# Twelve probability buffers, and fewer, longer value passes in two stages of a four-stage attention kernel

## The reference

```
x = x + masked_attention(layernorm(x))      # softmax over keys j >= i
x = x + ffn0(layernorm(x))                  # one of 8 matrices, picked by an argmax
x = x + rbf_attention(layernorm(x))         # exp(-sigma * |q - k|^2), no softmax
x = x + ffn0(layernorm(x))
x = x + relative_attention(layernorm(x))    # QK + uK + rel_shift(Qr + vr), softmax
x = x + ffn1(layernorm(x))
x = x + rope_attention(layernorm(x))        # rotated q and k, softmax
x = x + ffn1(layernorm(x))
```

## Time and profile before

| | |
|---|---|
| median of 3 runs | 2841.02 us |
| profiled execution | 2840.0 us, span 2838.2 us |
| PE busy | 2662.1 us (94%) |
| DVE busy | 2066.8 us (73%) |
| ACT busy | 2100.8 us (74%) |
| GpSimd busy | 905.8 us (32%) |
| value matmuls (L977) | 30208 instructions |

### The profile page before, as it was taken

One profiled execution on the slowest core, in us unless ns is written; L12 is line 12 of the kernel. 1 busy time (PEld: TensorE's weight loads), 2 busy tenths in 40 slices (PEclk: granted clock), 3 DMA queues, 4 the chain that ended last, 5 costly groups with the idle time before them and its releaser, 6 DMA issues.

```text
span 2838.2 us, 107110 instructions
## 1 busy us (share of the span) xinstructions
PE 2662.1 (94%) x43744; PEld 1599.3 (56%) x43744; DVE 2066.8 (73%) x5515; ACT 2100.8 (74%) x3766; POOL 905.8 (32%) x1609
## 2 busy tenths in 40 slices
PE   3999998999999999999999999999999999999995
PEld 1666565655555555666666666666644444444443
DVE  4888888822222228888788888878889989999992
ACT  1777776799999996666666666666678878888883
POOL 2212132322213242722541361252136134351231
PEclk7999999999999999999999999999999999999997
DMA  6333232334424351411331241222123223232121
GB/s 175 88 95 116 85 109 79 112 104 127 128 88 121 96 160 55 125 57 55 97 89 50 72 131 50 72 81 70 45 64 106 63 63 98 64 112 63 57 71 40
DMA packets 197778, 250.62 MB, mean 88 GB/s; under 512 B 48340, under 2 KB 113748, under 8 KB 197288
## 3 DMA queue, kind: packets, MB, share of 16 engines
q1 hardware_dynamic: 197288, 243.77, 29.2%
HBM read 133.28 MB, written 100.14 MB: 82 GB/s over the span
## 4 chain that ended last, share of the span: by engine, by line
PE 69%; DVE 20%; issue 5%; ACT 2%; SPq 2%; DMA 1%; POOL 1%; DVEq 0%; ACTq 0%; POOLq 0%
PE ppv L977 29%; DVE mx L1244 14%; PE ring L834 6%; PE ring L884 6%; PE ring L819 5%; PE ring L845 4%; PE ring L917 3%; PE pm L1013 2%; DVE seen L1228 2%; DVE seen L1239 1%; PE ring L933 1%; PE pm L998 1%; PE pm L1067 1%; PE pm L1058 1%; ACT probs L1118 1%
## 5 line engine op out<-in xcount | busy, mean ns | idle before, releaser
L1118 ACT ACTIVATE probs<-ring 128x512 f32<-128x512 f32 (+1 forms) x3280 | 1969.8, 684 | 662.9 <-PE ring L834 316.0
L1244 DVE TENSOR_REDUCE mx<-ring 128x1 f32<-128x512 f32 (+2 forms) x2112 | 1284.0, 649 | 241.7 <-PE ring L884 89.4
L977 PE MATMUL ppv<-probs,values 128*32 128x128 f32 x30208 | 1146.9, 278 | 7.3 <-POOL probs L1511 2.8
L977 PEld LDWEIGHTS ppv<-probs,values 128*32 128x32 f32 x30208 | 792.8, 109 | 321.2 <-issue 163.6
L1239 DVE CUSTOM_DVE_ANT_0 seen<-ring,low_seen 128x512 f32<-128x512 f32 x576 | 392.4, 681 | 72.0 <-PE ring L884 71.6
L891 PE MATMUL ring<-kst,qst 48*128 48x512 bf16 (+1 forms) x1060 | 362.6, 391 | 37.7 <-DMA kst<-records_k 20.0
L845 PE MATMUL ring<-qst,kst 51*128 51x512 bf16 (+2 forms) x1092 | 346.2, 385 | 15.8 <-issue 11.5
L1481 POOL CAST mparts<-mall 128x8 bf16<-128x8 f32 x192 | 36.6, 191 | 826.0 <-DVE mall L1262 700.6
L884 PE MATMUL ring<-kst,qst 112*128 112x512 bf16 (+3 forms) x768 | 251.6, 328 | 11.8 <-DVE mx L1228 6.7
L1511 POOL TENSOR_SCALAR_AFFINE_SELECT probs<-probs 128x512 f32<-128x512 f32 x128 | 81.3, 635 | 564.9 <-ACT probs L1118 352.0
L834 PE MATMUL ring<-qst,kst 115*128 115x512 bf16 (+3 forms) x768 | 250.9, 327 | 0.0
(11 more groups left out here) (165 smaller groups left out, 3002.5 us busy)
## 6 DMA issues: line engine op xcount, KB each, us to landing
qst<-records_q SPq DMA_DIRECT2D x448, 96.0 KB
heads_out<-osb SPq DMA_DIRECT2D x256, 128.0 KB, 2.0
kst<-records_k SPq DMA_DIRECT2D x320, 96.0 KB
records_k<-parts SPq DMA_DIRECT2D x96, 256.0 KB, 3.2
records_q<-parts SPq DMA_DIRECT2D x96, 256.0 KB, 3.4
kst<-records_k SPq DMA_DIRECT2D x128, 102.0 KB
oT<-heads_out SPq DMA_DIRECT2D x64, 128.0 KB, 2.7
den<-inverses SPq DMA_DIRECT2D x48, 128.0 KB, 2.6
```

What stands on the lines that cost most here:

```text
L977: mm = pe.matmul(ppv[32 * g:32 * g + 32, c:c + P], values[:, (n // H) % 2, v:v + 32], src[:, at * P:(at + 1) * P], start=u == 0 and qt < 4 ...
L1118: nc.scalar.activation(probs_of(rd.n, u), src, ACT.Exp, scale=1.0 if rd.s == RBF else SCALE).then_inc(s_exp, 1)
L1244: ins = dve.tensor_reduce(mx[:, slot, to:to + 1], bank[:, at * P:(at + nt) * P], AX.X, ALU.max)
```

## The change

NBUF goes from 8 to 12. In REL the four passes of a round become three, of seven, six and five units, behind slots 8, 14 and 20. In MASKED the three passes become two, of five and four units, behind slots 6 and 11. The number of value matmuls is the same. Two more things follow from NBUF: the buffer of a narrow unit is its number modulo 12, and in the first narrow round after the wide rounds of RBF the first 12 units, not the first 8, wait for the pass of the unit three to four before them. The wide rounds go on using the first eight buffers, in four pairs.

```diff
-NBUF = 8
+NBUF = 12
...
     if rd.s == REL:
-        return {6: [0, 1, 2, 3, 4], 10: [5, 6, 7], 14: [8, 9, 10, 11, 12], 20: [13, 14, 15, 16, 17]}
+        return {8: [0, 1, 2, 3, 4, 5, 6], 14: [7, 8, 9, 10, 11, 12], 20: [13, 14, 15, 16, 17]}
     if n == 9:
-        return {5: [0, 1, 2], 8: [3, 4, 5], 11: [6, 7, 8]}
+        return {6: [0, 1, 2, 3, 4], 11: [5, 6, 7, 8]}
```

## The result

In four runs of each, taking turns on one chip, the changed kernel took 2881.36 us (2875.85 to 2891.4) and the kernel before 2842.65 us (2840.93 to 2856.81): a ratio of 1.0134, interval 1.0103 to 1.0165. The forecast was 2849 us, the range ended at 2860. The sign was right, the size five times too small.

The account below looks back on a forecast made before the run. Quiet rounds were taken as a loop through PE and DVE, coupled by three PSUM banks. Terms +10.0 - 2 + 2.6 - 3.8 + 1 = +7.8 us gave 2847.8 in a profile, 2849 us as median; range 2825 to 2860.

Parts of the forecast that it names:

- Step 1: Buffers: twelve instead of eight bring nothing by themselves; they let passes wait longer.
- Step 2: PE: each pass costs 0.23 us beside its units; 64 masked and 64 relative rounds lose one each, 29.4 us.
- first rival: Whole kernel: PE is the bound and the switch price is simply saved, 29.4 us less, 2812 us; chance 10%.
- Step 3: Quiet relative rounds: new waits for DVE at slots 7 and 8 outweigh the saving; +0.25 us each, +10.0 for 40.
- Step 5: Quiet masked rounds: one DVE idle grows to 0.77 us, the other shrinks to 0.15; +0.08 each, +2.6 for 32.
- Steps 4 and 6: Loaded rounds: relative ones mostly escape new waits, -2 us; many masked ones save the full price, -3.8 us.
- Step 7: Seams at the first wide round and first narrow round after: each 0 to 0.8–1.2 us, together +1 us.
- last rival: Masked stage: passes outrun ScalarE, each waiting 0.3 us for an exponential; +19 us more, 2862 or more; chance 10%.

Follow-up runs that it names:

- e1: Kernel before with twelve buffers and all passes where they were: 2840.48 us against 2841.37, ratio 1.0000.
- e7: Changed kernel with maxima reading 32 columns of each bank and not subtracted, exponential scale 1e-6: 2725.59 us, ratio 0.9587 to the kernel before.
- e8: e7 with the relative stage's transpose moved to slot 8, beside the seven-unit pass: 2714.49 us, measured once.
- e4: Changed kernel with ScalarE's planned work of a slot, the emptying of pm in it, ahead of the exponential: 2870.71 us against 2842.87, ratio 1.0100.
- e5: Kernel before with ScalarE's planned work of a slot, the emptying of pm in it, ahead of the exponential: 2837.39 us, ratio 0.9983.
- e10: e7 with masked exponentials reading and writing 256 of 512 columns: 2711.69 us, measured once.
- v1: Kernel before with twelve buffers, emptying first, and four evener relative passes (first two of four units each): 2837.79 us against 2841.79, ratio 0.9988.
- v2: Kernel before with twelve buffers, emptying first, four evener relative passes, masked passes and eviction a slot later: 2842.91 us against 2844.03, ratio 0.9993.

## Why the prediction was wrong

**Step 1, buffers:** right (e1).

**Step 2, the price of a pass:** the 0.23 us is real on PE (0.21 from e7 to e8), but counted one time too many. I took it as saved in all 128 rounds; in the relative ones it had been shared with the transpose, and parting the two brings it back. So the first rival, 29 us of gain, was not to be had even with a quick DVE: with quick maxima the relative round is 13.76 either way, and the chance of 10% was generous. Step 3 did not suffer much, since it walked PE's own timeline.

**Step 3, quiet relative rounds:** right, mechanism and size: +0.21 us a round for +0.25. The waits at slots 7 and 8 were 0.14 and 0.16 for 0.22 and 0.17, the pass 1.67 for 1.67, DVE's idle before slot 9 1.15 for 1.04. One term of the walk was too small: it put slot 7 0.06 us behind the transpose, and it came 0.15 behind (1267.81 to 1267.96). The wait for DVE that follows is shorter by as much, so the sum did not feel it. e7 shows that it is DVE's loop: with quick maxima the loss is gone.

**Step 5, quiet masked rounds, is the step that failed first:** +13.1 us for +2.6. Its first half is right (0.82 idle for 0.77). The failing words are "the other idle shrinks to some 0.15, since slots 7 to 2 run with no pass between". The stretch ends at slot 3, not at slot 2. The second pass stands behind slot 2 and grew from three units to four; slot 3's item comes behind it, and that idle is 0.49. 6.08 + 0.82 + 0.49 gives 7.39 by the very method of the step; it was not taken round the whole loop. Nor was this pass priced: it takes 1.43 us, where the price of step 2 for four units gives 0.14 + 4 x 0.218 = 1.01.

**Steps 4 and 6, loaded rounds:** wrong in sign, +6.0 and +8.7 us for -2 and -3.8. "PE has no gap" was read as "PE saves the full price". A PE without gaps says that nothing makes it wait now, not how near the next wait is. In the masked stage it was in the emptying of `pm`, which the pass behind slot 8 had covered; e4 and e5 show that this is 5.5 of the 6.3 us that the 25 rounds at full clock lose. The rest of the masked row is the seam (1.6), and what the granted clock and the count of rounds make of it. In the relative stage the order gives back 2.6 us in the changed kernel (e4) but 1.6 in the kernel before too (e5), so about 1 of the 6.0 is its doing; the rest I put down to DVE's loop, since with quick maxima 1.6 is left, but no single wait of it was traced.

**Step 7, seams:** the first wait came as the step has it, between the last two masked evictions (8.94 us for 7.37, in the loaded row of the table). ACT of the changed kernel, then of the kernel before, at the first wide exponentials:

```profile
604.38 2.85 ACT L1118 ACTIVATE probs<-ring 128x1024 f32<-128x1024 f32 x3 [1.64 <-PE ppv L977]
```

```profile
580.10 2.86 ACT L1118 ACTIVATE probs<-ring 128x1024 f32<-128x1024 f32 x3 [0.74 <-PE ring L819]
```

It cost 1.6 us, where the step allowed 1.2 at the most. The other +4.7, and the 2.5 before the first eviction, the step did not have. Much of it goes with the granted clock: 0.83 from 605 to 615 us, where the same place before (580 to 590) had 1.00, and 0.79 from 1118 to 1126 for 1.00 (1091 to 1099). e4, with the same passes and the clock at 1.00, takes 6.49 us from the last masked eviction to the first of RBF, as the kernel before does, and the changed kernel takes 7.86. What set the clock back in these places was not tried; it stays open. The second seam of the step, at the end of RBF, costs nothing that shows (501.7 for 501.9).

The last rival, passes that outrun ACT, had the right engine and the wrong place. In the rounds read here no pass waits inside for an exponential; ACT holds up PE's scores through the ring (e7, e10) and the projections through the emptying (e4). Its 2862 was nearest to the 2881 of all that was listed. Of the 38.7 us, then: quiet rounds of both stages 21.5, loaded masked 8.7 (a seam of 1.6 in it), loaded relative 6.0, the rest the other seams and the clock. The trace's differences add up to 43, since the profiled execution of the changed kernel, 2883.0 us, lies 1.6 above its median, and that of the kernel before 2.7 below the median here.

The Trainium skill (Perfetto Trace Analysis, Matmul Optimizations) wants matmuls back to back in batches, because the matmul engine scales its power with its utilization. Here the granted clock was already 1.00 in the quiet rounds of both kernels and 0.99 over the masked stage, so the longer batches had nothing to win, and they cost 1.3%. Its other advice there, to use all 8 PSUM banks, is followed already: six in `ring`, and `pm` and `ppv`. PE's passes turn into idle time at the two rings of three; no run had a larger ring.

## What to carry to other kernels

When a producer serves engines through a ring of a few banks and goes away for a burst, go once round the whole loop for each served engine: burst, plus the time until its next item, less the work that the ring holds for it; a burst that the ring's work does not cover leaves such an idle, and lengthening one at the edge of its cover gives the added length as idle (v1: 0.22 us more of pass, 0.21 of idle). A saved switch is worth nothing if another instruction beside it was sharing its price. A burst can also cover another engine's work: before taking it away, ask what is done beneath it. Here it was an emptying of PSUM that stood in program order behind an exponential; putting it in front took the wait away. And before two sums of rounds are called equal, look at the granted clock of each round in them.

## What was unexpected of the hardware

- A transpose of 24 weight columns between bf16 score matmuls costs PE 0.25 us beyond the 0.22 us steps of its neighbours, as much as a pass of f32 value matmuls costs beside its units; next to each other they cost it once (13.76 and 13.55 us a round, e7 and e8).
- The DMA that places the maxima is close behind PE: with masked rounds of 6.85 us instead of 7.02, PE's weight loads waited for it 27 times (15.7 us) where it had been twice (4.4 us).
- Twelve executions of one kernel (v2) on one chip lay between 2829.5 and 2850.6 us and almost in the order of their mean granted clock, 0.979 down to 0.970. Which stretches ran at the lower level differed from kernel to kernel, and one such stretch made two sums of rounds equal that were not (e4 and e5).
